# A new set-up ahead of a two-layer LSTM: other orders of loads, products and conversions on every queue

## The chip, the cores and the metric

One core of one Trainium2 chip. The metric is the device time of one execution in microseconds (us). The kernel before takes 1119.18 us (median of 3 runs, 1118.47 to 1119.56). "Before" and "after" are the kernel without and with the change; line numbers (L1069) are those of the kernel before.

## The reference, cut to what matters

2048 sequences of 10 steps. Table rows are looked up, projected and convolved over time; with a tanh'ed embedding they feed two LSTM layers (H = 256, 8 steps) and three dense layers without a nonlinearity between them.

```python
rp = concat([region_tbl[region_idx], poi_tbl[poi_idx]])          # (2048, 10, 12)
nv = concat([rp @ W_rp + b_rp, coords @ W_co + b_co])            # 40 features
conv = elu(conv1d(nv, conv_w) + conv_b)                          # 3 taps, 32 channels, 8 steps
emb = tanh(concat([car_tbl[car_idx], week_tbl[week_idx], time_tbl[time_idx]]))   # 27
x = concat([conv, broadcast(emb)])                               # (2048, 8, 59)
h = lstm_layer(x, Wih0, Whh0, ...); h = lstm_layer(h, Wih1, Whh1, ...)
y = ((h[:, -1] @ W1 + b1) @ W2 + b2) @ W3 + b3
```

## The kernel before, in words

The 2048 sequences are four batches of 512 columns. Ahead of the batches stands a **set-up**, written out by hand for each engine, that does once what all batches need. Then each engine walks through the same list of stages (`stages`): cells of layer 0 and layer 1 in turn, and between them the turning of gathered rows, the convolution and the embeddings' share of the gates of the next batch. A cell is 8 gate tiles (6 in a sequence's first step) of 128 rows by 512 columns; a recurrent tile is six fp16 matmuls (weights and states split into a high and a low part) after the input's matmul.

The set-up, on the tensor engine (PE), in its order: W1 turned (8 matmuls, L1233); the product W1·W2 in eight column blocks (`product_w12`, L1069, each 8 matmuls of 257 columns), with `band` between the fourth and fifth (24 small matmuls, L1109: projection folded into the convolution's weights); `product_conv_bias`; `poi_rows` (80 matmuls of 12 columns, L1130: batch 0's point-of-interest rows by a one-hot product); `turn_wx` (L1098: the input weights turned and scaled by a diagonal); batch 0's first rows turned and the first convolution half (`conv_pair(0)`, L1166), around `turn_wh(0)` (L1084: the recurrent weights of layer 0, four quarters of 8 matmuls); the embeddings turned; the **first cell**; the embeddings' gates (`emb_product`, L1174) between two head products (`product_head`, (W1·W2)·W3, L1139, 16 matmuls of 512 columns each); `conv_pair(1)`; `turn_wh(1)` and `turn_wh(2)`, layer 1's weights; `sum_head_bias`; the **second cell**, from which on the steady order runs.

The scalar engine (ACT) takes products out of the accumulators: `put_w12`, `put_wx_hi`, `put_wh_hi` (L624), `put_head_hi`, the convolution's elu parts, the cells' gates (L683), `put_emb_gates` (L666). The vector engine (DVE) does index arithmetic (`indices`), the one-hots, `row_maxima` (L780) and `row_scales` for the scaling diagonals, the low parts (`put_wh_lo` L814, `put_wx_lo`, `put_head_lo`), the rest of the elu, and the head bias sum (L845). SyncE (SP) issues the loads in order and then, in `put_pair`, the copies of the convolution's results into `x_in`: 12 DMAs for the first two steps, 12 for the next two. GpSimd (POOL) gathers table rows by indirect DMA (L527): batch 0's regions of four steps, after a wait the embeddings' rows, then the other steps.

What orders the engines is semaphores alone: each engine runs its own list in order, so a waiting instruction holds all behind it on its engine.

Of the kernel before, what the change touches and what calls it, by code (L numbers as in the profile page):

```python
# [33 lines left out]
SIDES = 2  # L34

# [132 lines left out]
def build(nc, d):  # L168
# [33 lines left out]
    with ExitStack() as ctx:  # L202
# [3 lines left out]
        def sem(name):  # L206
            return ctx.enter_context(nc.semaphore(name))

        idx_raw = {"region": sb("region_raw", [P, NB * GR, T], I32), "poi": sb("poi_raw", [P, NB * GR, T], I32),
                   "car": sb("car_raw", [P, NB * GR, 1], I32), "week": sb("week_raw", [P, NB * GR, 1], I32),  # L210
                   "time": sb("time_raw", [P, NB * GR, 1], I32)}
        idx_wrap = sb("idx_wrap", [P, NB * GR, T], F32)
        idx = {k: sb(f"{k}_idx", list(v.shape), F32 if k == "week" else I32) for k, v in idx_raw.items()}
# [40 lines left out]
        with ExitStack() as early:  # L254
            PAD = (WIN - 1) * D_FEAT
            proj_t = sb("proj_t", [D_NV, PAD + D_FEAT + PAD], F32, early)
            conv_w = sb("conv_w", [D_NV, TAPS, D_CONV], F32, early)
            proj_bias = sb("proj_bias", [D_NV, 1], F32, early)
            conv_b = sb("conv_b", [P, 1], F32, early)
            poi_sum = sb("poi_sum", [P, GR * T, D_POI], F32, early)  # L260
            poi_tbl = sb("poi_tbl", [P, D_POI], F32, early)
            poi_rest = sb("poi_rest", [P, 2, D_POI], F32, early)
            poi_part = sb("poi_part", [P, 3, D_POI], BF16, early)
            poi_number = sb("poi_number", [P, 2], F32, early)
# [28 lines left out]
        with ExitStack() as before_layer1:  # L293
            w_nat.extend(sb(f"w_nat{i}", [P, M, H], F32, before_layer1) for i in (1, 2))
            diag.append(sb("diag1", [P, M, P], F32, before_layer1))
            w12_t = sb("w12_t", [P, K2, H], F32, before_layer1)
# [12 lines left out]
        idx_in = {k: sem(f"{k}_in") for k in idx_raw}  # L309
        coords_in = sem("coords_in")  # L310
# [4 lines left out]
        proj_in, conv_bias_in = sem("proj_in"), sem("conv_bias_in")  # L315
# [7 lines left out]
        zeroed, proj_zeroed = sem("zeroed"), sem("proj_zeroed")  # L323
# [5 lines left out]
        poi_part_step, poi_part_put = sem("poi_part_step"), sem("poi_part_put")  # L329
# [5 lines left out]
        diag_ready, wh_acc, wh_hi_put, wh_lo_put = sem("diag_ready"), sem("wh_acc"), sem("wh_hi_put"), sem("wh_lo_put")  # L335
        wx_copied = sem("wx_copied")
        wx_acc, wx_hi_put, wx_lo_put = sem("wx_acc"), sem("wx_hi_put"), sem("wx_lo_put")
        emb_copied = sem("emb_copied")
        band_acc, band_put = sem("band_acc"), sem("band_put")
# [3 lines left out]
        head_acc, head_hi_put, head_low_put = sem("head_acc"), sem("head_hi_put"), sem("head_low_put")  # L343
        one_ready, head_sum_step, head_bias_acc, head_bias_put = (sem("one_ready"), sem("head_sum_step"),
# [10 lines left out]
        x_put = [sem("x0_put"), sem("x1_put"), sem("x2_put")]  # L355

# [26 lines left out]
        WH_BANKS = ((1, 2, 0, 1), (1, 0, 2, 1), (0, 2, 1, 3))  # L383
# [4 lines left out]
        PAIR_DMAS = 3 * PAIR * 2  # L388

        def x_count(part, n):  # L390

            return ((n * 3 + PAIR_DMAS) * DMA, (n * 3 * (TT - 1) + PAIR_DMAS) * DMA, (n + 1) * (3 * TT * DMA))[part]

# [23 lines left out]
        def put_pair(eng, s):  # L417
            for k in range(PAIR):
                for half in range(2):
                    row = (half * PAIR + k) * D_CONV  # L420
                    put_x(eng, s * PAIR + k, slice(row, row + D_CONV), slice(s * HALF, (s + 1) * HALF),
                          slice(half * HALF, (half + 1) * HALF), x_put[s])

        @block.sync
        def _(sp):
# [4 lines left out]
            def load_rows(k):  # L430
                load(idx_raw[k][:, :, :].rearrange("p (n g) t -> p n g t", g=GR),
                     d[f"r_{k}_idx"].rearrange("(n p g) t -> p n g t", p=P, g=GR), idx_in[k])
# [4 lines left out]
            load(w2[:, :, 0:D2 // 2], w2_rows[:, :, 0:D2 // 2], w2_in[0])  # L437
            for k in ("car", "time", "week"):
# [47 lines left out]
        def _(pool):  # L486
# [29 lines left out]
            for n in range(NB):  # L516
# [56 lines left out]
                else:  # L573

                    for c in range(CH):
                        pool.wait_ge(turned[c], n)
# [766 lines left out]
```

## Time and profile before

| | us |
|---|---|
| median of 3 runs | 1119.18 |
| the profiled execution: its time | 1118.79 |
| its span (first to last instruction) | 1117.0 |
| PE busy | 1076.6 (96%) |
| DVE, ACT, POOL busy | 743.0, 510.1, 319.9 |
| PE's first matmul of the second cell starts at | 102.10 |

The span is the stretch from the first to the last instruction; the time adds what lies around it (1.79 us). PE's busy time is summed over matmuls whose ends are modelled; a busy PE is not PE at its peak.

### The profile page before, as it was taken

The page shows a single profiled execution, that of the slowest core. Times are in us where ns is not written, and L with a number is a line of the kernel's source. Part 1 is how long each engine was busy: PE and PEld are TensorE (multiplying, and loading weights), DVE is VectorE, ACT ScalarE, POOL GpSimd, SP SyncE. Part 2 cuts the span into 40 slices and gives each one's busy share as a digit, 9 for nine tenths or more (in the row PEclk, how much of TensorE's full clock was granted, in tenths as well). Part 3 has the DMA queues.
Part 4 walks back from the last instruction along what each step waited for, and adds up shares of the span by engine and source line. Part 5 has one row for each costly group of instructions (what it writes and reads, how often), then busy time and mean ns, then how long its engine had stood idle before and what let it go on. Part 6 is the DMA issues. An engine that isn't in the chain of part 4 may idle for free.

```text
span 1117.0 us, 14516 instructions
## 1 busy us (share of the span) xinstructions
PE 1076.6 (96%) x4994; PEld 520.8 (47%) x4994; DVE 743.0 (67%) x1136; ACT 510.1 (46%) x735; POOL 319.9 (29%) x338
## 2 busy tenths in 40 slices
PE   5959999999999999999999999999999999999998
PEld 4835444444444544444444544444444544444444
DVE  1558858576676767666686768666676758666653
ACT  1334544444455544444455544444455545444432
POOL 6550025562540015562541015552442000000000
PEclk9779999999999999999999999999999999999999
DMA  9510001000010101000010101000010100000001
GB/s 224 144 17 15 1 2 30 3 2 1 2 31 1 40 2 31 3 2 1 2 30 2 40 1 29 5 2 1 2 30 1 38 1 21 9 0 1 0 1 38
DMA packets 34382, 22.59 MB, mean 20 GB/s; under 512 B 22922, under 2 KB 27018, under 8 KB 34186
## 3 DMA queue, kind: packets, MB, share of 16 engines
q1 hardware_dynamic: 21648, 20.54, 6.7%
q0 software_dynamic: 9984, 1.12, 2.6%
q8 instruction: 41, 0.67, 0.2%
q10 hardware_dynamic: 2682, 0.04, 0.2%
q14 instruction: 27, 0.22, 0.1%
HBM read 11.18 MB, written 4.19 MB: 14 GB/s over the span
## 4 chain that ended last, share of the span: by engine, by line
PE 93%; DVE 3%; issue 1%; DMA 1%; ACT 1%; SPq 1%; ACTq 0%; DVEq 0%
PE acc L1224 52%; PE acc L1215 28%; PE acc L1206 5%; PE acc L1069 2%; PE aux L1314 2%; PE acc L1139 1%; DMA w<-in_L_rec_W 1%; PE aux L1174 1%; SPq L413 1%; PE aux L1304 1%; ACT gates L683 1%; PE aux L1130 0%; PE aux L1098 0%; PE aux L1084 0%; DVE gates L925 0%
## 5 line engine op out<-in xcount | busy, mean ns | idle before, releaser
L1224 PE MATMUL acc<-h_part,wh 128*128 128x512 f16 (+1 forms) x2688 | 656.1, 380 | 1.6 <-DVE h_part L976 1.6
L1224 PEld LDWEIGHTS acc<-h_part,wh 128*128 128x128 f16 x2688 | 245.2, 98 | 322.0 <-issue 55.7
L1215 PE MATMUL acc<-h_part,wh 128*128 128x512 f16 (+1 forms) x1488 | 358.9, 379 | 0.4 <-issue 0.3
L683 ACT ACTIVATE gates<-acc,gate_bias,unscale 128x512 f32<-128x512 f32 x254 | 196.1, 777 | 328.9 <-PE acc L1224 278.0
L683 ACT ACTIVATE gates<-gates,gate_bias,unscale 128x512 f32<-128x512 f32 x242 | 190.2, 811 | 150.1 <-DVE gates L925 143.8
L1215 PEld LDWEIGHTS acc<-h_part,wh 128*128 128x128 f16 x1488 | 144.4, 98 | 178.2 <-issue 7.6
L527 POOL DMA_INDIRECT feat<-in_L_rec_region_tbl,region_idx x160 | 160.4, 1002 | 163.7 <-PE acc L1224 124.7
L925 DVE TENSOR_TENSOR gates<-acc,emb_gates 128x512 f32<-128x512 f32 x242 | 161.6, 686 | 54.9 <-PE acc L1224 46.3
L527 POOL DMA_INDIRECT feat<-in_L_rec_poi_tbl,poi_idx x120 | 121.7, 1014 | 114.5 <-PE acc L1224 96.9
L1206 PE MATMUL acc<-x_in,wx 96*128 96x512 f32 (+1 forms) x248 | 139.2, 567 | 15.7 <-DMA x_in<-conv_hi 11.9
L972 DVE TENSOR_TENSOR h_full<-gates,tanh_c 128x512 f32<-128x512 f32 x120 | 82.6, 688 | 75.8 <-ACT tanh_c L688 69.6
L951 DVE TENSOR_TENSOR cell_c<-gates,cell_c 128x512 f32<-128x512 f32 x112 | 76.8, 686 | 76.4 <-ACT gates L683 72.6
L946 DVE TENSOR_TENSOR ig<-gates 128x512 f32<-128x512 f32 x112 | 76.9, 687 | 67.2 <-ACT gates L683 64.3
L688 ACT ACTIVATE tanh_c<-cell_c 128x512 f32<-128x512 f32 x128 | 80.0, 625 | 59.9 <-DVE cell_c L954 42.2
L976 DVE TENSOR_TENSOR h_part<-h_full,h_part 128x512 f16<-128x512 f32 (+1 forms) x120 | 83.3, 694 | 16.0 <-DVE h_part L973 6.2
L954 DVE TENSOR_TENSOR cell_c<-cell_c,ig 128x512 f32<-128x512 f32 x112 | 77.5, 692 | 13.1 <-DVE cell_c L951 1.8
L973 DVE TENSOR_TENSOR h_part<-gates,tanh_c 128x512 f16<-128x512 f32 (+1 forms) x120 | 83.0, 692 | 0.0
L1206 PEld LDWEIGHTS acc<-x_in,wx 96*128 96x128 f32 x248 | 47.9, 193 | 47.1 <-issue 17.1
L539 POOL COPY feat<-coords 128x80 f32<-128x80 f32 x4 | 1.0, 252 | 220.9 <-PE aux L1152 218.4
L897 DVE RECIPROCAL neg_part<-neg_part 128x512 f32<-128x512 f32 (+1 forms) x9 | 27.0, 2997 | 0.3
L1314 PE MATMUL aux<-w_head,h_last 128*128 128x512 f32 x96 | 24.1, 404 | 0.6 <-DVE h_last L967 0.6
L944 DVE TENSOR_TENSOR cell_c<-gates 128x512 f32<-128x512 f32 x16 | 11.0, 689 | 14.7 <-ACT gates L683 13.5
(126 smaller groups left out, 375.4 us busy)
## 6 DMA issues: line engine op xcount, KB each, us to landing
out<-y SPq DMA_DIRECT2D x16, 256.0 KB, 2.6
x_in<-conv_hi SPq DMA_DIRECT2D x56, 64.0 KB
feat<-in_L_rec_region_tbl,region_idx POOLq DMA_INDIRECT x160
w<-in_L_rec_W SPq DMA_DIRECT2D x2, 1024.0 KB
w_nat<-in_L_rec_Whh SPq DMA_DIRECT2D x2, 1024.0 KB, 13.1
w<-in_L_rec_W SPq DMA_DIRECT2D x1, 2048.0 KB
feat<-in_L_rec_poi_tbl,poi_idx POOLq DMA_INDIRECT x120
x_in<-conv_lo SPq DMA_DIRECT2D x28, 64.0 KB
```

Source lines behind the costliest of these rows:

```text
L527: pool.indirect_dma_start(out, None, tables[k], bass.IndirectOffsetOnAxis(ap=idx[k][:, n * GR + g, t:t + 1], axis=0)).then_inc(landed, DMA)
L683: nc.scalar.activation(gates[layer][:, j, g, :], source, ACT.Tanh if g == GATE_G else ACT.Sigmoid, bias=gate_bias[:, layer, m:m + 1], scal ...
L688: nc.scalar.activation(tanh_c[layer][:, j, :], cell_c[layer][:, j, :], ACT.Tanh).then_inc(tanh_c_done[layer], 1)
L925: nc.vector.tensor_tensor(gates[0][:, j, g, :], acc[:, s.bank(j, g), :], emb_gates[:, g * HK + j, :], ALU.add).then_inc(gate_sum, 1)
L946: nc.vector.tensor_tensor(ig[:, j, :], i_gate, g_gate, ALU.mult).then_inc(ig_done[layer], 1)
L954: nc.vector.tensor_tensor(c, c, ig[:, j, :], ALU.add).then_inc(c_done[layer], 1)
L972: nc.vector.tensor_tensor(h_full[:, j, :], o_gate, th, ALU.mult).then_inc(h_full_done[layer], 1)
L973: nc.vector.tensor_tensor(hi, o_gate, th, ALU.mult).then_inc(h_hi_done[layer], 1)
L976: nc.vector.tensor_tensor(lo, h_full[:, j, :], hi, ALU.subtract).then_inc(h_done[layer], 1)
L1206: mm = nc.tensor.matmul(bank, wx[:, rows], x_in[:, s.t, :], start=True, stop=s.first and not s.opening)
L1215: mm = nc.tensor.matmul(bank, wh[:, 1, a, c, rows], h_part[0][:, s.write_slot, b, c, :], start=(c == 0 and a == b == HI), stop=(s.first an ...
L1224: mm = nc.tensor.matmul(bank, wh[:, own_w, a, c, rows], h_part[layer][:, s.read_slot, b, c, :], start=False, stop=(c == HK - 1 and a == LO))
```

## The change

The same work is computed with other instructions and another order in the set-up; the steady stages are as before. The parts:

- **Loads.** Batch 0's region indices and coordinates are loaded alone, the other batches' at the end of SP's loads. Rows are grouped by 128 neighbours (`"(g p) t -> p g t"`), so one partition's run of indices is 40 bytes. Car, time and week indices come as 16 rows of 512 bytes each, one tile of 96 rows, whose wrap-around is computed at once and which PE turns (`turn_small`). W2's two halves go together ahead of the poi indices; W3 goes ahead of the biases and of layer 1's weights.
- **Projection and band.** The weights are loaded in natural order three times on a diagonal and turned by PE (`turn_proj`); the band is 4 matmuls over all taps, and the convolution's bias one.
- **Poi rows.** 20 matmuls of 24 columns with a block-diagonal table.
- **W12.** ACT takes out all 257 columns in one copy; the bias is added by DVE once (`add_head_bias`). The order is blocks 0, 1, band, blocks 2 to 7.
- **Order on PE.** `turn_wh(0)` runs mostly ahead of the first rows' turning; both head products and `turn_wh(1)` run ahead of the first cell, all three `emb_product` parts and `turn_wh(2)` after it.
- **Order on DVE and ACT.** `row_maxima(1)` and `(2)` run after the first elu; layer 1's diagonal is built by ACT (8 activations) in place of one DVE instruction; the head bias sum is split in two; `elu(1)` runs after `put_wh_lo(2)`.
- **The opening's copies.** The first cell waits only for its own step's six copies (`x_put[0]`); the six of the second step have a semaphore of their own.
- **Gathers.** POOL issues the embeddings' gathers without waiting for the first 16 region gathers to land.
- **Index arithmetic** of batches 1 to 3 (region and poi, two rounds of three) stands after the second cell on DVE, where poi's one round stood.

```diff
@@ SP
-            load_rows("region")
+            load(idx_raw["region"][:, 0:GR, :], rows_of("r_region_idx", 0, GR), first_idx_in)
+            sp.wait_ge(small_zeroed, 1)
+            for k, at in (("car", CAR_AT), ("time", TIME_AT), ("week", DAY_AT)):
+                load(small_raw[at:at + NB * GR, :], d[f"r_{k}_idx"].rearrange("(g p) -> g p", p=P), small_idx_in)
             load(w1_nat[:, :, :], d["W1"].rearrange("(a p) n -> p a n", p=P), w1_in)
...
+            load(w3[:, :, :], d["W3"].rearrange("(k p) n -> p k n", p=P), w3_in)
...
+            load(idx_raw["region"][:, GR:NB * GR, :], rows_of("r_region_idx", GR, NB * GR), later_idx_in)
+            load(idx_raw["poi"][:, GR:NB * GR, :], rows_of("r_poi_idx", GR, NB * GR), later_idx_in)
+            load(coords[:, GR:NB * GR, :], coord_rows[:, GR:NB * GR, :], later_coords_in)
@@ POOL
                     copy_coords()
-                    pool.wait_ge(rows_first_in, GR * PAIR_WIN * DMA)
-                    pool.wait_ge(idx_ready, 3)
-                    gather_emb()
+                    pool.wait_ge(small_put, 1)
+                    gather_emb(0, GR)
                     copy_emb()
@@ ACT
+            def diagonal1():
+                act.wait_ge(prep, 9)
+                for m in range(M):
+                    nc.scalar.activation(diag[1][:, m, :], ident[:, :], ACT.Copy, scale=row_scale[:, 1, m:m + 1]
+                                         ).then_inc(diag_ready[1], 1)
...
             put_wx_hi()
+            put_wh_hi(0, 0, 3)
             put_turned(feat_t[0:KP, 0, :], aux[0:KP, 0, :], first_turned, 1, first_turned_put)
-            put_wh_hi(0, 0, 1)
+            put_wh_hi(0, 3, 4)
             elu_parts(0, slice(0, HALF))
-            put_wh_hi(0, 1, 4)
-            emb_tanhs(0, acc[:, 3, :])
-            act.wait_ge(prep, 4)
+            put_head_hi(0)
+            diagonal1()
+            put_head_hi(1)
+            emb_tanhs(0, acc[:, 0, :])
+            put_wh_hi(1)
             act.wait_ge(bias_ready, 1)
             first, second = opening_cells(STEPS)
             cell_acts(first)
-            put_emb_gates(0, 0)
-            put_head_hi(0)
-            put_emb_gates(0, 1)
+            for part in range(3):
+                put_emb_gates(0, part)
+            put_wh_hi(2)
             put_turned(feat_t[0:KP, 1, :], acc[0:KP, 0, :], turned[0], 1, turned_put[0])
-            put_head_hi(1)
             elu_parts(1, slice(0, HALF))
-            put_emb_gates(0, 2)
-            put_wh_hi(1)
-            put_wh_hi(2)
             cell_acts(second)
@@ DVE, the order after
+            indices(0, "region", REG, slice(0, GR), (first_idx_in, DMA))
+            small_indices()
             put_band()
+            put_conv_bias()
+            poi_parts()
             poi_one_hot()
             row_maxima(0)
             row_scales(0)
+            week_lookup()
             put_poi()
             put_wx_lo()
+            add_head_bias()
+            put_wh_lo(0)
...
             elu(0, slice(0, HALF), (0, slice(0, HALF)), ())
+            sum_head_bias(0, K2 // 2)
+            put_head_lo(0)
+            row_maxima(1)
+            row_maxima(2)
+            row_scales(1)
+            put_head_lo(1)
             split_emb(0)
+            put_wh_lo(1)
             first, second = opening_cells(STEPS)
             cell(first)
+            sum_head_bias(K2 // 2, K2)
+            put_wh_lo(2)
             elu(1, slice(0, HALF), (0, slice(HALF, NCOL)), ())
...
             cell(second)
-            indices(4, "poi", POI)
+            dve.wait_ge(x_second_put, HALVES_DMAS * DMA)
+            later = slice(GR, NB * GR)
+            indices(1, "region", REG, later, (later_idx_in, 2 * DMA))
+            dve.wait_ge(idx_ready, 2)
+            indices(2, "poi", POI, later, (later_idx_in, 2 * DMA))
@@ PE, the order after
+            turn_small()
...
+            turn_proj()
...
+            product_w12(0)
+            product_w12(1)
+            band()
+            for m in range(2, K2):
                 product_w12(m)
             poi_rows()
+            turn_wx([(band_put, 1), (conv_bias_put, 1), (conv_bias_put, 1), (poi_put, SIDES)])
+            turn_wh(0, [(wx_lo_put, 1), (wx_lo_put, 2), (wx_lo_put, 4)])
             pe.wait_ge(rows_first_in, GR * PAIR_WIN * DMA)
             pe.wait_ge(coords_put, 1)
+            pe.wait_ge(wh_lo_put, 1)
             turn_steps(aux[:, 0, :], 0, PAIR_WIN, first_turned)
+            turn_wh(0, [(wh_lo_put, 2)], begin=3)
...
             conv_pair(0)
+            product_head(0)
+            product_head(1)
             pe.wait_ge(emb_copied, 1)
+            turn_emb(acc[:, 0, :])
+            turn_wh(1, [(wh_lo_put, 3), (wh_lo_put, 4), (first_turned_put, 1), (relu_done, 1)])
             pe.wait_ge(emb_ready, 2)
             cell(first)
+            pe.wait_ge(wh_lo_put, 7)
+            for part in range(3):
+                if part:
+                    pe.wait_ge(emb_gates_put, EMB_BEFORE[part])
+                emb_product(0, part)
+            turn_wh(2, [(wh_lo_put, 8), (emb_gates_put, 5), (emb_gates_put, 7), (emb_gates_put, M)])
             pe.wait_ge(rows_in[0], rows_count(0, 0))
             turn_steps(acc[:, 0, :], PAIR, PAIR_WIN, turned[0])
+            sum_head_bias()
             pe.wait_ge(turned_put[0], 1)
+            pe.wait_ge(wh_lo_put, 9)
             conv_pair(1)
             cell(second)
```

In `cell`, the second cell's first three tiles wait for the first cell's gates or the turned rows, and its fourth (place 3) for `head_bias_put`, DVE's reading of that accumulator bank.

## Rows read from the trace of the kernel before

**Rows 1.** PE's longest wait behind 103 us: us in total, times, longest.
```profile
PE acc L1206 <- ACT gates L683: 2.7, 3, 0.9
```

**Rows 2.** Timeline of PE in the set-up: start us, elapsed us, engine, line.
```profile
7.58 1.94 PE L1233 MATMUL acc<-ident,w_nat 128*128 128x128 f32 x8 [7.58 <-DMA w_nat<-in_L_rec_W]
11.04 10.18 PE L1069 MATMUL acc<-w_t,w 128*128 128x257 f32 x32 [1.52 <-DMA w<-in_L_rec_W]
21.15 1.69 PE L1109 MATMUL aux<-conv_w,proj_t 40*84 40x32 f32 x19
...
27.89 8.61 PE L1069 MATMUL acc<-w_t,w 128*128 128x257 f32 x32
...
42.30 2.90 PE L1130 MATMUL aux<-poi_part,poi_hot 64*64 64x12 bf16 x46 [1.02 <-issue]
45.13 6.70 PE L1098 MATMUL aux<-diag,wx_rep 128*96 128x128 f32 x32
...
52.10 1.06 PE L1084 MATMUL aux<-diag,w_nat 128*128 128x128 f32 x8
...
69.82 0.76 PE L1206 MATMUL acc<-x_in,wx 96*128 96x512 f32 x1 [11.87 <-DMA x_in<-conv_hi]
...
75.80 7.03 PE L1139 MATMUL acc<-w,w_t 128*128 128x512 f32 x16
...
102.10 0.79 PE L1206 MATMUL acc<-x_in,wx 96*128 96x512 f32 x1
...
113.09 0.58 PE L1206 MATMUL acc<-x_in,wx 96*128 96x512 f32 x1
```

**Rows 3.** Timelines of SP and ACT: two loads, the input weights' copies.
```profile
1.25 0.50 SPq L428 DMA_DIRECT2D w_nat<-in_L_rec_W  x1
...
17.60 4.33 SPq L428 DMA_DIRECT2D coords<-in_r_coords  x1
...
36.95 1.64 ACT L700 COPY wx_rep<-wx_nat 128x768 f32<-128x768 f32 x2
```

**Rows 4.** Stretches: PE, PEld, DVE, ACT, POOL busy; PE clock, DMA share, GB/s.
```profile
30.00:32.00 2.00, 2.00 (x9) 1.65 (x9) 1.97 (x2) 0.54 (x2) 1.12 (x1) 0.82 0.61 5
...
46.00:48.00 2.00, 2.00 (x11) 2.00 (x10) 0.47 (x2) 0.58 (x1) 1.52 (x3) 0.50 0.00 0
...
60.00:62.00 2.00, 0.00 (x0) 0.00 (x0) 2.00 (x5) 0.00 (x0) 1.65 (x2) 0.86 0.13 21
...
78.00:80.00 2.00, 2.00 (x6) 0.90 (x5) 1.90 (x4) 0.24 (x1) 1.07 (x2) 1.00 0.00 0
```

**Rows 5.** Groups, 0 to 103 us: busy us, mean ns, idle.
```profile
L814 DVE TENSOR_TENSOR wh<-aux,wh 128x512 f16<-128x512 f32 x12 | 7.9, 686 | 1.5 <-ACT wh L624 1.5
L780 DVE TENSOR_REDUCE row_max<-w_nat 128x8 f32<-128x2048 f32 x3 | 6.8, 2280 | 0.0
L845 DVE SCALAR_TENSOR_TENSOR head_sum<-w,b,head_sum 128x512 f32<-128x512 f32 x7 | 5.3, 752 | 0.2
...
L683 ACT ACTIVATE gates<-acc,gate_bias,unscale 128x512 f32<-128x512 f32 x6 | 4.4, 774 | 11.8 <-PE acc L1209 11.8
L666 ACT COPY emb_gates<-aux 128x512 f32<-128x512 f32 x8 | 4.2, 594 | 0.0
...
L617 ACT ACTIVATE b<-acc,b_col 128x1 f32<-128x1 f32 x8 | 2.2, 270 | 0.0
```

**Rows 6.** Timeline of DVE: first elu's ends, the poi indices' last.
```profile
56.21 0.28 DVE L894 TENSOR_SCALAR neg_part<-tanh_part 128x256 f32<-128x256 f32 x1
...
59.62 0.43 DVE L911 TENSOR_TENSOR conv_lo<-relu_part,conv_hi 128x256 fp32r<-128x256 f32 x1
...
121.65 0.24 DVE L758 TENSOR_SCALAR poi_idx<-idx_wrap 128x160 int32<-128x160 f32 x1
```

**Rows 7.** Timeline of POOL: the copy that follows the embeddings' gathers.
```profile
45.74 0.51 POOL L555 COPY emb<-emb 128x384 f32<-128x384 f32 x1 [4.41 <-DMA emb<-in_L_rec_time_tbl,time_idx]
```

**Rows 8.** Timeline of PE behind the second cell: the only stall there.
```profile
129.37 0.49 PE L1206 MATMUL acc<-x_in,wx 96*128 96x512 f32 x1 [0.46 <-DVE gates L925]
```

More of the change, by code:

```diff
@@ L418, in put_pair @@
             for k in range(PAIR):
+                put = x_put[1] if s else (x_put[0], x_second_put)[k]
                 for half in range(2):
@@ L541, in copy_coords, with gather_emb @@
                                           ).then_inc(coords_put, 1)
-                def gather_emb():
-                    for g in range(GR):
-                        gather("car", emb[:, g, 0, 0:D_CAR], g, 0, emb_rows_in)
-                        gather("time", emb[:, g, 0, D_CAR + D_WEEK:D_EMB], g, 0, emb_rows_in)
+                def gather_emb(begin, end):
+                    for g in range(begin, end):
+                        for k, at, cols in (("car", CAR_AT, slice(0, D_CAR)),
+                                            ("time", TIME_AT, slice(D_CAR + D_WEEK, D_EMB))):
+                            at += n * GR + g
+                            gather(k, emb[:, g, 0, cols], small_idx[:, at:at + 1], emb_rows_in)
                 def copy_emb():
@@ L615, in put_w12 @@
                 act.wait_ge(w12_acc, m + 1)
-                nc.scalar.copy(w12_t[:, m, 0:H], bank[:, 0:H]).then_inc(w12_put, 1)
-                nc.scalar.activation(b12[:, m:m + 1], bank[:, H:H + 1], ACT.Identity,
-                                     bias=b2_col[:, m:m + 1]).then_inc(w12_put, 1)
+                nc.scalar.copy(w12_t[:, m, :], bank[:, 0:H + 1]).then_inc(w12_put, 1)
             def put_wh_hi(i, begin=0, end=len(QUARTERS)):
@@ L1102, in turn_wx, with turn_small, turn_proj @@
                     mm.then_inc(wx_acc, 1)
+            def turn_small():
+                pe.wait_ge(small_ready, 1)
+                nc.tensor.transpose(acc[:, 3, 0:SMALL], small_wrap[:, :], ident[0:SMALL, 0:SMALL]
+                                    ).then_inc(small_turned, 1)
+            def turn_proj():
+                rows, cols = BIAS_AT + 1, TAPS * D_NV + 1
+                pe.wait_ge(proj_in, (2 * TAPS + 2) * DMA)
+                nc.tensor.transpose(aux[0:cols, 1, 0:rows], proj_nat[:, :], ident[0:rows, 0:rows]
+                                    ).then_inc(proj_turned, 1)
@@ L1111, in band @@
                 mm.then_inc(band_acc, 1)
[L1113 to L1119 removed]
+                nc.tensor.matmul(aux[:, 1, P:P + 1], conv_w[:, :, :].rearrange("k s o -> k (s o)"), proj_bias[:, :],
+                                 start=True, stop=True).then_inc(conv_bias_acc, 1)
```

313 lines of the change are left out of this document (160 added, 153 removed).

## The prediction

> **What bounds the kernel now.** I read PE's waits behind the set-up first, since the change leaves the steady stages alone. The longest sum there is 2.7 us in a thousand [rows 1]: from the second cell on PE is never short of work, so every microsecond by which that cell starts earlier or later moves the end by about as much. The question is therefore one number, the start of the second cell, 102.10 before [rows 2].
>
> Next PE's timeline of the set-up [rows 2]. Three things are to be seen in it. First, small matmuls are dear: `band` has 24 of them, 19 take 1.69 us together and the rest stretch to 27.89, 6.7 us from 21.15, with the engine idle and waiting for nothing that the profile names ("issue"); `poi_rows` has 80 and ends at 45.13, though its last 46 ran in 2.90. Second, a hole from about 58 to 69.82: the first elu and twelve copies into `x_in`, 11.87 us of idle [rows 2]. Third, two head products of 7.03 us each stand behind that hole, in front of the second cell. Then the clock [rows 4]: full (2.4 GHz) in 78 to 80 with PE busy, half (1.2 GHz) in 46 to 48 although PE is busy, after the sparse poi rows, and falling in 60 to 62 after PE had been idle since 58.
>
> The sum below is made in the profiled execution's own time: 1118.79 us, 0.39 under the median of the three runs, span 1117.0.
>
> **Stage A: from the start to the last of `turn_wx`** (51.8 before: 45.13 + 6.70).
> - W1's load is issued behind three more loads at 0.50 each [rows 3], so PE turns W1 from about 8.9 in place of 7.58 and W12 starts at 12.2 (before 11.04). This is a loss of 1.2. `turn_small` (one matmul) ends before W1 lands; `turn_proj` is one more.
> - A 512-column fp32 product costs 7.03/16 = 0.44 us a matmul at full clock, so 257 columns cost 0.22 at full and 0.43 at half. Before, 32 took 10.18 [rows 2], about half of them at 0.43. After, I put all 16 of blocks 0 and 1 at 0.43: 6.9, to 19.1.
> - `band` and bias: 4 + 1 products, 10 matmuls (fp32 goes in two) at 0.09 (1.69/19): 0.9, to 20.0. Bounds: 0.9, and 0.9 + 3.8 if the idle pieces of before come back.
> - Six blocks at full clock: 48 x 0.22 = 10.3, to 30.5. DVE's line beside it: band copy, poi parts, one-hots, `row_maxima(0)` 2.28 [rows 5] and the diagonal end some 11 us behind the band, at 31, in time.
> - `poi_rows`: 20 matmuls. The nearest row is 46 in 2.90, 0.06 each, with 64 by 64 tiles at half clock; for twice the width I take 0.10, 2.0 us, beside ACT's last W12 copy and the two copies of the input weights, 0.6 + 1.64 [rows 3]. `turn_wx` starts at 33.
> - `turn_wx`, 32 matmuls: 6.70 before at half clock; 4 x 1.06 = 4.2 at full, by the eight of `turn_wh` [rows 2]. I expect the clock to hold, since PE's gaps are now short. With 1.8 kept for idle pieces of the kind above, the stage ends at T = 39. Bounds: 37.4 without them, 45 with both old stalls and the half clock. Gain in A: 12.8.
>
> **Stage B: from T to the second cell** (50.3 before: 51.8 to 102.1). Times are after T.
> - `turn_wh(0)`'s three quarters 3.2, first rows turned 3.8, last quarter 4.9, `conv_pair(0)` 5.5. ACT's three activations to 6.6, DVE's elu 3.84 (56.21 to 60.05, [rows 6]) to 10.5. Before, the elu ended at 60.05, 8.3 behind 51.8: the four low parts that now stand ahead of it cost 2.
> - This loss is covered. PE does both head products meanwhile: 5.5 + 2 x 7.0 = 19.4. The copies of the first step land at about 10.5 + 6 x 0.64 + 2.6 = 17 (an estimate from the 9.8 us that the twelve took from 60.05 to 69.82 [rows 2]). The hole is gone; what is late next is layer 1's diagonal.
> - DVE behind the elu: half of the head sum 2.9 (0.75 each), a low part 0.7, two maxima 4.6 [rows 5], scales 1.1: 19.8. ACT's 8 activations of 128x128: between 0.27 (one column) and 0.59 (512 columns) each [rows 5], I take 0.28: 2.2 (bounds 2.2 and 4.7), to 22.0. PE idles 2 us there. `turn_wh(1)` 4.2 to 26.2.
> - ACT takes out those quarters until 26.8, then six gates at 0.77 and two tanh: 5.5, to 32.3. PE's first cell ends at 28.8; the first part of `emb_product` at 29.5; the next needs banks that ACT empties after its gates: 3 x 0.51, 33.9. In this gap of 4.4 us the clock falls, as it did 4 us into the hole at 60 to 62 [rows 4]. Parts 2 and 3, then `turn_wh(2)` at 1.6 a quarter (6.70/4, the half clock's price) in place of 1.06: to 43. Turned rows, bias sum, `conv_pair(1)`: second cell at 44.5. Bounds: 42.2 (clock held) and 48 (dear activations too).
> - Gain in B: 50.3 - 44.5 = 5.8.
>
> **Behind the start, two losses.** `elu(1)` now stands ahead of DVE's reading of the head bias's bank. ACT's parts end at about 45.5, the elu 3.84 later, the bias 0.68 after it, at 50, whereas PE wants that bank for place 3 at 44.5 + 3 x 1.57 = 49.2 (a tile is a seventh of 113.09 - 102.10, [rows 2]): 0.8 to 1.2 lost; I take 1.1. DVE's index arithmetic behind the cell is two rounds where one ended at 121.89 [rows 6]; PE was already short of DVE by 0.46 at 129.37 [rows 8], so the added round, 0.7 to 1.0, goes straight into that stall: 0.8.
>
> **Cost nothing.** The wait that POOL drops: without it the embeddings' gathers start some 2 us earlier (a guess: the coordinates, which POOL copies first, land at about 28). Their copy was ready at 46.25 [rows 7], and PE turns them at T + 19.4 = 58. With the wait left in, it would be ready 12 us early all the same. The waits between later steps stay; the second turning is at 81. W3 and layer 1's weights: 10.6 MB landed by 46 before, and the maxima want theirs at 53.
>
> Sum: 12.8 + 5.8 - 1.1 - 0.8 = 16.7. 1118.79 - 16.7 = 1102.1 profiled, **1102.5** against the median.
>
> **Rivals.**
> 1. *The idle pieces come back* (they are the loads' traffic in PE's way, not the count of small matmuls): band + 3.8, `poi_rows` + 2.7 less the 1.8 allowed, half clock in `turn_wx` + 2.5, some 1.5 more for blocks at half clock: 8.7 less gained, 1111. For it: they stand where DMA is busiest, and it is as busy after. Against: the big matmuls of W12 show none in the same traffic. Chance 0.13.
> 2. *Everything holds*: no idle pieces (1.6 to 1.8 more) and no fall of the clock in B (2.3 more): 1098.4. Chance 0.13.
> 3. *Slower: late weights of layer 1.* `turn_wh(1)` now stands in front of the first cell, so Wih1 and Whh1, which end SP's weights behind W3 and the biases, must land before anything goes on. Each us beyond T + 14 = 53 costs one; slower than before from a landing at 53 + 17 = 70, and at 75 the time is 1124. For it: row loads of short runs choke SP (coordinates in 80-byte runs held it for 4.33, [rows 3]) and 30 to 32, in the biases' 4-byte runs, moved 5 GB/s [rows 4]. Against: DMA was idle at 46 to 48 with the same bytes [rows 4], 22 us short of the point. Chance 0.04.
>    The Trainium skill, "DMA: Bandwidth & Descriptors", Specifications, says that a transfer wants 512 B at least for line rate. The change goes from 160-byte runs to 40-byte ones for the indices, which speaks against it. The slump at 30 to 32 agrees in kind. By that page alone, with each of the 4,608 late runs (1,536 each for region, poi and coordinates) charged as 512 B, they are 2.4 MB, an estimate of 8 us; they stand behind all weights, so the sum is the same unless their like stands ahead.
> 4. *The change does nothing for the end*, because the second cell's start is tied to something that I don't see: 1118 to 1120. Chance 0.02.
>
> **How the numbers follow.** The forecast has 0.68. Its own range is 1097.5 to 1107 from the bounds: T + 3 or - 1.6, B + 3 or - 2.3. To hold the time 8 times in 10, I reach to the first rival's near side: 1097 to 1110. What a measurement can tell from no change is 0.2%, 2.2 us. Faster: 0.68 + 0.13 + 0.13 = 0.94; same 0.02; slower 0.04.
>
> **What would show it.** In the profile after: the last of `turn_wx` at 37 to 41; head products side by side from about 44 to 58 and no hole for `x_in` ahead of the first cell; about 2 us of idle PE ahead of `turn_wh(1)`; half clock in `turn_wh(2)`; the second cell at 83 to 84, with about 1 us of idle at its fourth tile; a stall of about 1.3 us where 129.37 stood. Wrong would be a second cell later than 90 or earlier than 79, a wait for a weights' DMA, or a gather that ends a wait of PE.

## The result, and the profile after

| | median us | lowest to highest | runs |
|---|---|---|---|
| before | 1120.03 | 1118.34 to 1121.56 | 20 |
| after | 1115.78 | 1105.89 to 1119.75 | 20 |

The ratio is 0.9959, 95% interval 0.9945 to 0.9972: faster, by 4.3 us, where 16.7 was forecast (1102.5, range 1097 to 1110). Eighteen of the 20 executions of the changed kernel took 1114.76 to 1119.75; the other two took 1105.89 and 1109.16, and have no trace. The profiled execution took 1114.92 us, span 1113.1.

PE's timeline of the set-up after the change (start us, elapsed us, engine, line, operation; in brackets the idle time before it and what ended it). It answers to [rows 2].

```profile
9.63 6.10 PE L1144 MATMUL acc<-w_t,w 128*128 128x257 f32 x16
...
20.21 1.30 PE L1196 MATMUL aux<-conv_w,proj_t 120*84 120x32 f32 x8 [4.47 <-issue]
...
21.75 8.02 PE L1144 MATMUL acc<-w_t,w 128*128 128x257 f32 x29
...
34.14 0.38 PE L1144 MATMUL acc<-w_t,w 128*128 128x257 f32 x1 [2.42 <-issue]
...
39.66 6.46 PE L1144 MATMUL acc<-w_t,w 128*128 128x257 f32 x16 [5.14 <-ACT w_t L658]
45.95 1.27 PE L1209 MATMUL aux<-poi_block,poi_hot 128*128 128x24 bf16 x20
48.12 3.77 PE L1173 MATMUL aux<-diag,wx_rep 128*96 128x128 f32 x32 [0.89 <-ACT wx_rep L740]
...
73.75 3.81 PE L1159 MATMUL aux<-diag,w_nat 128*128 128x128 f32 x32 [2.49 <-issue]
...
85.18 0.96 PE L1253 MATMUL aux<-emb_in,we 128*128 128x512 f32 x3 [4.11 <-ACT emb_gates L706]
...
88.35 5.96 PE L1159 MATMUL aux<-diag,w_nat 128*128 128x128 f32 x32
...
96.11 0.49 PE L1289 MATMUL acc<-x_in,wx 96*128 96x512 f32 x1
...
101.85 0.49 PE L1289 MATMUL acc<-x_in,wx 96*128 96x512 f32 x1 [0.84 <-DVE b_head L1105]
```

`turn_wx` ends at 48.12 + 3.77 = 51.9, as before (51.8), and not at 39. The second cell starts at 96.11, 6.0 earlier. In the prediction's two stages: A gained nothing (12.8 forecast), B takes 44.2 in place of 50.3 (44.5 forecast). Behind the second cell the span goes on for 1017.0 where it was 1014.9: 2.1 lost, 1.9 forecast.

Why A is long is seen on the other engines: first ACT's and VectorE's timelines after the change, then POOL's.

```profile
16.60 0.37 ACT L658 COPY w_t<-acc 128x257 f32<-128x257 f32 x1 [2.81 <-PE acc L1144]
39.14 1.20 ACT L658 COPY w_t<-acc 128x257 f32<-128x257 f32 x4 [22.17 <-remote]
```

```profile
29.23 0.29 DVE L884 COPY conv_band<-aux 84x128 f32<-84x128 f32 x1 [23.37 <-remote]
32.06 0.16 DVE L888 COPY conv_bias<-aux 128x1 f32<-128x1 f32 x1 [2.54 <-remote]
```

```profile
23.55 0.94 POOL L549 DMA_INDIRECT feat<-in_L_rec_region_tbl,region_idx  x1 [0.30 <-issue]
25.32 0.25 POOL L561 COPY feat<-coords 128x80 f32<-128x80 f32 x1 [0.83 <-issue]
25.73 0.97 POOL L549 DMA_INDIRECT emb<-in_L_rec_car_tbl,small_idx  x1 [0.16 <-issue]
...
34.49 2.59 POOL L549 DMA_INDIRECT emb<-in_L_rec_time_tbl,small_idx  x1 [0.30 <-issue]
```

ACT takes W12's third block only at 39.14 and then four at once, although PE had finished that block by about 25; "remote" says that the profile finds nothing on this core that it waited for. VectorE copies the band, done at 21.5, at 29.23. PE, out of accumulator banks, stands still for 5.14, and for 2.42 with nothing named ("issue"). I call these the *pieces*: idle time for which the profile names no cause on this core. POOL's gathers now run from 4.67 to 37.08, with no break longer than the 1.24 us between the two rows of gathers. The same marks were in the profile of before, and I had passed over them: ACT's third block copy was late there by a "remote" too, but came at 27.62, 2.7 us behind POOL's last region gather (24.95) (its row, kernel before):

```profile
27.62 0.37 ACT L616 COPY w_t<-acc 128x256 f32<-128x256 f32 x1 [8.63 <-remote]
```

### The profile page after: what moved, and what is told of

Same layout as the page of the kernel before. It is cut to its first block, busy times and chain, and to the rows that moved or that the text cites. A ratio compares the mean times of both kernels' runs of the same rounds, so it can differ in the third digit from the quotient of the medians.

```text
span 1113.1 us, 14344 instructions
## 1 busy us (share of the span) xinstructions
PE 1071.6 (96%) x4898; PEld 515.2 (46%) x4898; DVE 741.6 (67%) x1146; ACT 510.7 (46%) x737; POOL 319.5 (29%) x339
## 3 DMA queue, kind: packets, MB, share of 16 engines
q10 hardware_dynamic: 2327, 0.08, 0.2%
## 4 chain that ended last, share of the span: by engine, by line
PE 86%; DVE 5%; issue 2%; SPq 2%; another core or an unknown queue 2%; ACT 2%; DMA 1%; DVEq 0%; ACTq 0%
PE acc L1307 48%; PE acc L1298 25%; PE acc L1289 5%; SPq L428 2%; PE aux L1396 2%; PE acc L1218 1%; PE acc L1144 1%; PE aux L1159 1%; DVE neg_part L967 1%; ACT gates L723 1%; PE aux L1253 1%; DVE h_full L1042 1%; DVE h_part L1043 1%; DVE gates L995 1%
## 5 line engine op out<-in xcount | busy, mean ns | idle before, releaser
L1289 PEld LDWEIGHTS acc<-x_in,wx 96*128 96x128 f32 x248 | 47.1, 190 | 38.9 <-issue 7.0
L1144 PE MATMUL acc<-w_t,w 128*128 128x257 f32 x64 | 21.7, 506 | 8.8 <-ACT w_t L658 5.1
```

Source lines behind the costliest of these rows:

```text
L1289: mm = nc.tensor.matmul(bank, wx[:, rows], x_in[:, s.t, :], start=True, stop=s.first and not s.opening)
```

## The experiments

Eighteen runs were made on four chips, A to D. This can't be left out: the kernel before took 1119.8 us on A, 1107.7 on B, 1107.7 and 1108.1 in the two sets on C, and 1120.7 on D. Which chip gave the result above is not on record; its kernel before took 1120.0, as on A and D. Only C was used in two sets, so a cause that came with a set and not with the chip is not excluded. Each ratio is to the kernel before in the same set; edits are to the changed kernel. T is the end of `turn_wx`, S the start of the second cell, both from the one execution that was profiled; the us are medians of four to six executions (e10: one).

### Chip A: traffic, the biases, POOL's wait, conv_w

```diff
# e1_hold: ahead of W3's load, SP's queue
+            sp.wait_ge(w12_put, K2)
# e2_bias_runs: the biases in runs of 128 B, not 4 B, into other places
-                    load(bias_in[:, layer, i, :], d[f"{k}{layer}"].rearrange("(m p) -> p m", p=P), bias_loaded)
+                    row = (layer * 2 + i) * 32
+                    load(bias_in[row:row + 32, :, :, :].rearrange("p a b m -> p (a b m)"),
+                         d[f"{k}{layer}"].rearrange("(a b) -> a b", b=32), bias_loaded)
# e3_wait_back: ahead of gather_emb(0, GR)
+                    pool.wait_ge(rows_first_in, GR * PAIR_WIN * DMA)
# e4_conv_w_first: conv_w's and conv_b's loads first on ACT's queue
```

> The changed kernel with one added wait: SP issues W3 and everything behind it (biases, layer 1's weights, later rows) only once ACT has taken out all eight W12 blocks. Theory F (in the changed kernel ACT, DVE and PE stand still between 17 and 39 us because what they need next of their own code arrives late while the loads keep the DMA engines busy; ACT takes out the third W12 block at 39.1 though PE had it done at about 24): DMA falls quiet at about 26 us, ACT's third copy comes at 24 to 30, turn_wx ends at 38 to 44, the time is 1101 to 1108. Rival D (the 4,096 four-byte bias runs choke the rings; they come later here too): the same gain at the front. Rival S (ACT's late copies have to do with its own place in the order and not with traffic): ACT's third copy stays at 35 or later and the time at 1114 or above, since the loads are now later still.

> The changed kernel with the four bias loads as 32 runs of 128 bytes each in place of 1,024 of 4 bytes, into other places of the tile (the gate biases are not those of the reference); all else as it was, W3 still ahead. Theory F: bulk bytes stay the same, so ACT's idle before its third W12 copy stays above 8 us, the time moves by less than 5 us (1111 to 1116). Rival D (small runs, not bytes): ACT's third copy comes before 30 and the time falls to 1103 to 1108.

> The changed kernel with POOL's wait for the first 16 region gathers put back ahead of the embeddings' gathers. The prediction's step (this wait costs nothing, hidden by 12 us): ratio to the changed kernel within 0.3%, 1113 to 1118, embeddings' copy still bound by DVE's day lookup at 44 us. Rival (gathers that pile up in the rings are what holds the others' code back): the time moves by more than 5 us and ACT's idle before its third W12 copy shrinks by as much.

> The changed kernel with the convolution's weights as the first two loads of ACT's queue, ahead of b1 and the projection. PE idles 4.5 us ahead of the band (15.7 to 20.2) and no releaser is named. Theory C (that wait is for the convolution's weights, whose 128-byte runs share the DMA engines with the poi indices' 10 KB runs): the band starts at 15.8 to 16.5 and the 4.5 us of idle are gone. If C is the whole cause of the late stage A, the time falls to 1105 or less; if theory F holds beside it, ACT's copies stay late (behind 33 us) and the time falls by 0 to 5 us. Theory F alone: the band still waits until about 20.

| | us | ratio, interval | T | ACT's third block |
|---|---|---|---|---|
| e1_hold | 1114.26 | 0.9939 [0.9917, 0.9962] | 50.9 | 39.07 |
| e2_bias_runs | 1114.83 | 0.9963 [0.9951, 0.9975] | 51.1 | 39.10 |
| e3_wait_back | 1107.53 | 0.9901 [0.9885, 0.9917] | 43.9 | 27.95 |
| e4_conv_w_first | 1112.79 | 0.9919 [0.9889, 0.995] | 51.5 | 38.93 |

e2 leaves the biases in the wrong places, so its gates are computed with other numbers than the reference's; it serves for its time alone. e1 and e4 scatter as the changed kernel does: e1 from 1107.51 to 1116.12, e4 from 1103.92 to 1117.90, and e4's trace is of its slowest execution.

The traffic of W3, the biases and layer 1's weights is not the cause: e1 takes it out of that stretch (windows of 28 to 34 us, after and then e1: us, busy time of PE, PEld, VectorE, ACT and POOL, PE's clock, DMA share, GB/s), and ACT is as late. What e1 leaves is the traffic up to about 25 us (192 GB/s from 18 to 25). Nor are the biases' short runs the cause.

```profile
28.00:34.00 6.00, 2.52 (x11) 1.76 (x10) 1.89 (x11) 0.00 (x0) 4.53 (x5) 1.00 0.88 155
```

```profile
28.00:34.00 6.00, 3.37 (x15) 2.30 (x13) 3.13 (x11) 0.00 (x0) 4.53 (x5) 0.93 0.11 5
```

POOL's wait makes the difference: with it T is 43.9 and the time 1107.53, 5 to 7 us under its neighbours, and its ratio's interval (0.9885 to 0.9917) lies clear of that of the changed kernel in the result (0.9945 to 0.9972). It is not clear of e4's, whose executions scatter most. ACT's, POOL's, VectorE's and PE's timelines of e3:

```profile
27.95 0.65 ACT L659 COPY w_t<-acc 128x257 f32<-128x257 f32 x2 [10.28 <-PE acc L1145]
```

```profile
24.91 0.25 POOL L561 COPY feat<-coords 128x80 f32<-128x80 f32 x1 [0.42 <-issue]
30.07 2.80 POOL L549 DMA_INDIRECT emb<-in_L_rec_car_tbl,small_idx  x1 [4.90 <-DMA feat<-in_L_rec_region_tbl,region_idx]
```

```profile
27.82 0.29 DVE L885 COPY conv_band<-aux 84x128 f32<-84x128 f32 x1 [21.95 <-remote]
...
37.19 1.22 DVE L863 TENSOR_TENSOR diag<-ident,row_scale 128x1024 f32<-128x1024 f32 x1
```

```profile
38.52 5.40 PE L1174 MATMUL aux<-diag,wx_rep 128*96 128x128 f32 x32 [2.79 <-issue]
```

ACT is back 3.5 us behind the last region gather (24.49), and before the gathered rows have all landed, for which POOL waits until 30.07. A piece is left: VectorE's band copy comes at 27.82, so its chain ends with the diagonal at 38.41, and `turn_wx` starts right behind that, 2.8 us late and then partly at the half clock (5.40 us; 3.77 in e9 below). In e4 the 4.5 us of idle ahead of the band are gone, so they were conv_w's late landing, but in the execution profiled the pieces take all of it back (PE and ACT of e4):

```profile
16.02 0.72 PE L1196 MATMUL aux<-conv_w,proj_t 120*84 120x32 f32 x8
```

```profile
38.93 1.20 ACT L658 COPY w_t<-acc 128x257 f32<-128x257 f32 x4 [19.29 <-remote]
```

### Chip B: other pauses

```diff
# e5_pause_for_act: between region rows' and embeddings' gathers
+                    pool.wait_ge(w12_put, 3)
# e6_pause_early: the same wait after 12 of the 16 region gathers
# e7_gathers_late: ahead of all of POOL's gathers
+                    pool.wait_ge(w12_put, K2)
# e8_busy_pause: no wait; between the gathers 14 chained
+                        nc.gpsimd.memset(busy[:, :], 0.0).then_inc(busy_step, 1)
```

> The changed kernel with POOL waiting, between the region gathers and the embeddings' gathers, until ACT has taken out three W12 blocks. Theory P (ACT, and DVE too, get what they stand still for only while POOL pauses in its row of gathers; a pause of about 2.7 us is enough): ACT's third copy comes at 27 to 28.5 in place of 39.1, POOL's embeddings' gathers start right behind it, the time is 1105 to 1109 as with the old wait. Rival T (the third copy comes when the gathers' rows have landed, whatever POOL does): the third copy comes at 30 or later. Rival W (the old wait helps by the later start of the embeddings' gathers themselves, for DMA): time above 1110.

> The changed kernel with a pause of POOL after 12 of the 16 region gathers, at about 19.6 us, until ACT has taken out three W12 blocks; no pause behind the 16. Theory P: ACT is free at 22 to 23 and its third copy comes as soon as PE has the block, at 24 to 26, DVE's band copy at 21.5 to 23 in place of 27.8 or 29.2; the time is 1101 to 1107. Rival T or W (landing, or the embeddings' gathers): ACT's third copy not before 27.6, and the time 1107 or above.

> The changed kernel with all of POOL's gathers held until ACT has taken out all eight W12 blocks. Theory P at its purest: no idle of ACT or DVE is left in the first 30 us that is not explained by PE or a load (band copy 0.1 us behind the band, third copy as soon as the block is done, eighth at 31 to 34). The rows then come late: 16 gathers until about 53, landed at 56, so the first convolution waits for them and the time is 1108 to 1116. Rival F (the loads' traffic alone holds the engines): ACT's third copy still at 28 or later.

> The changed kernel with 14 chained clears of a spare tile of 256 columns on POOL between the two rows of gathers, about 5 us, so that POOL is busy there but issues no gather. If it is POOL's gathers that hold the others (their descriptors), ACT's third copy comes at 27 to 28.5 and the time is 1106 to 1110, as with the old wait; if it is any work of POOL, ACT's third copy stays at 38 or later and the time is at 1114 or above.

| | us | ratio, interval | T | S |
|---|---|---|---|---|
| e5_pause_for_act | 1100.72 | 0.9937 [0.9924, 0.9951] | 40.2 | 83.69 |
| e6_pause_early | 1102.11 | 0.9948 [0.9934, 0.9961] | 40.6 | 84.68 |
| e7_gathers_late | 1118.19 | 1.0095 [1.008, 1.011] | 40.1 | 101.31 |
| e8_busy_pause | 1101.35 | 0.994 [0.9924, 0.9957] | 40.3 | 83.81 |

No piece is in any of the four traces, and in e5 and e8 none is there even before POOL's pause begins at about 25, so they settled nothing about pauses. They raised the question whether this chip has pieces at all. What e7 shows is the price of too late a gather (its PE timeline), the case in which POOL's rows become the bound:

```profile
56.85 1.06 PE L1232 MATMUL aux<-ident,feat 128*56 128x128 f32 x4 [14.11 <-DMA feat<-in_L_rec_region_tbl,region_idx]
```

### Chip C: both kernels without the pieces

Unaltered: the changed kernel (e9), the kernel before (e10, one execution), e5 again (e11) and e3 again (e12).

> The changed kernel itself, unaltered, run beside the kernel before, the kernel with the old wait and the kernel with POOL's pause, all on one chip, because the kernel before took 1119.8 us on the chip of the first four experiments and 1107.7 on that of the next four. Theory G (POOL's unbroken row of gathers itself holds up the other engines' instructions: ACT's third block copy came at 39 and not at 25): wherever this runs, ACT's copy is again near 39, turn_wx ends at 51 to 52, and it is 8 to 12 us above the two kernels with a pause: ratio 0.995 to 0.997 on a chip like the first, about 1.003 on one like the second. Rival H (the hold-up is the chip's, not the gathers'): on a chip like the second ACT's copy comes at 25, turn_wx ends at 40 to 41 with no pause at all, the time is within 2 us of the kernels with a pause, about 1101, ratio 0.994; on a chip like the first it is 1114 to 1116 as before.

> The kernel before, unaltered, for its trace on this chip. Both theories: on a chip like the first turn_wx ends at 51.8 and there are pieces of idle time of PE in the set-up's first 40 us (ACT's copy 8.63 us behind, VectorE's conv_bias 3.07). Rival H: on a chip like the second (time near 1107.7) these pieces are absent, and turn_wx ends some 10 to 12 us earlier, at 40 to 42; Theory G keeps turn_wx at 48 to 52 and must find the 12 us elsewhere.

> The changed kernel with POOL waiting for ACT's third block copy (w12_put at 3) between the region rows' gathers and the embeddings', as once before, now on the same chip as the changed kernel. Theory G: ACT's copy at 25 to 28, turn_wx ends at 40 to 44, ratio 0.989 to 0.994 and 8 us or more under the changed kernel. Rival H: equal to the changed kernel within 2 us, in whichever state the chip puts both; on a chip like the first ACT's copy would then be late and the time 1112 or more.

> The changed kernel with the old wait back (POOL waits until the region rows have landed before the embeddings' gathers), now beside the changed kernel. Theory G: 6 to 10 us under the changed kernel, as the 8 us measured before. Rival H: that 8 us was the chip's own scatter; equal to the changed kernel within 2 us.

| | us | ratio, interval | T | S | span behind S |
|---|---|---|---|---|---|
| before (e10) | 1106.6 | | 40.5 | 89.96 | 1014.8 |
| after (e9) | 1101.05 | 0.9941 [0.9927, 0.9954] | 40.5 | 84.10 | 1015.2 |
| e11, pause for ACT | 1100.62 | 0.9929 [0.9916, 0.9943] | 39.8 | 84.10 | 1014.7 |
| e12, old wait | 1101.7 | 0.9946 [0.9932, 0.9959] | 39.8 | 83.06 | 1014.7 |

PE of the kernel before on this chip, then PE and ACT of the changed kernel:

```profile
11.64 8.83 PE L1069 MATMUL acc<-w_t,w 128*128 128x257 f32 x32 [1.97 <-ACT w_t L693]
20.40 1.98 PE L1109 MATMUL aux<-conv_w,proj_t 40*84 40x32 f32 x24
22.31 7.22 PE L1069 MATMUL acc<-w_t,w 128*128 128x257 f32 x32
...
30.01 4.92 PE L1130 MATMUL aux<-poi_part,poi_hot 64*64 64x12 bf16 x80
34.86 5.69 PE L1098 MATMUL aux<-diag,wx_rep 128*96 128x128 f32 x32
...
57.90 0.76 PE L1206 MATMUL acc<-x_in,wx 96*128 96x512 f32 x1 [10.21 <-DMA x_in<-conv_hi]
```

```profile
20.25 1.30 PE L1196 MATMUL aux<-conv_w,proj_t 120*84 120x32 f32 x8 [5.35 <-DMA conv_w<-in_L_rec_conv_b]
...
21.80 12.88 PE L1144 MATMUL acc<-w_t,w 128*128 128x257 f32 x48
34.52 1.28 PE L1209 MATMUL aux<-poi_block,poi_hot 128*128 128x24 bf16 x20
36.69 3.77 PE L1173 MATMUL aux<-diag,wx_rep 128*96 128x128 f32 x32 [0.89 <-ACT wx_rep L740]
```

```profile
25.61 0.37 ACT L658 COPY w_t<-acc 128x257 f32<-128x257 f32 x1 [10.29 <-PE acc L1144]
```

Compare with [rows 2]: the 24 small `band` matmuls take 1.98 here and 6.7 there, the 80 poi matmuls 4.92 in one run. So the idle between them is no property of the matmuls: the same instructions run without it here. And T is the same for both kernels here too, because the changed one waits 5.35 for conv_w and then begins W12's 48 at the half clock (1.2 GHz; 12.88 us for all 48, where e14 below took 10.69). A window of e9, columns as above:

```profile
20.00:24.00 4.00, 3.75 (x15) 3.39 (x16) 1.98 (x11) 0.00 (x0) 3.09 (x4) 0.50 1.32 235
```

That is the price of the gap ahead of it. The wait that POOL dropped makes no difference on this chip: e12's interval and the changed kernel's overlap.

### Chip C again: conv_w

> conv_w's and conv_b's loads first on ACT's queue, and POOL waiting for ACT's third block copy between the two rows of gathers. Theory (two separate losses in stage A: conv_w's late load, 5.35 us of PE's idle time ahead of the band, and, on a chip that shows them, the idle pieces, about 8 us): on a chip like the second turn_wx ends at 36 to 37 (40.5 less some 4 to 5, as the band then starts at 15 to 16) and the time is 4 us under the changed kernel, 1096 to 1098, ratio 0.990; on a chip like the first turn_wx ends at 38 to 40, ratio 0.986. Rival (W12's last rows of W3 or ACT's copies end later than PE and take its place): turn_wx stays at 39 to 41, ratio 0.9935.

> conv_w's and conv_b's loads first on ACT's queue, no pause: as e4, now on this chip. Theory: on a chip like the second it equals e13 (no pieces to lift), 4 us under the changed kernel's 1101; on one like the first it is 1110 to 1114, far above e13. Rival: no better than the changed kernel, ratio 0.994.

> The changed kernel with fourteen chained memsets on POOL between the region rows' gathers and the embeddings', now perhaps on a chip that shows the idle pieces. If only the pause in the gathers counts: as the old wait, ratio 0.989 to 0.991 there. If POOL must stand still: ACT's third copy waits until 38 to 40 and the ratio is 0.994 to 0.997. On a chip like the second: 0.994 as before, which tells nothing of it.

> The changed kernel with POOL waiting for ACT's third block copy between the two rows of gathers. On a chip like the first: ACT's copy at 27 to 29, turn_wx at 42 to 45, ratio 0.989 to 0.992 as the old wait gave. On a chip like the second 0.993 to 0.994.

| | us | ratio, interval | T | S |
|---|---|---|---|---|
| e13, conv_w first and e5's pause | 1096.11 | 0.9897 [0.9882, 0.9912] | 35.9 | 79.37 |
| e14, conv_w first alone | 1095.68 | 0.9899 [0.9884, 0.9914] | 34.6 | 78.05 |
| e15, as e8 | 1100.89 | 0.9937 [0.9923, 0.995] | 40.3 | 84.36 |
| e16, as e5 | 1100.57 | 0.9937 [0.9923, 0.995] | 39.8 | 83.06 |

PE of e14:

```profile
17.33 0.72 PE L1196 MATMUL aux<-conv_w,proj_t 120*84 120x32 f32 x8
...
18.10 10.69 PE L1144 MATMUL acc<-w_t,w 128*128 128x257 f32 x48
28.63 1.28 PE L1209 MATMUL aux<-poi_block,poi_hot 128*128 128x24 bf16 x20
30.80 3.77 PE L1173 MATMUL aux<-diag,wx_rep 128*96 128x128 f32 x32 [0.89 <-ACT wx_rep L740]
```

Two loads moved to the front of ACT's queue are worth 5 us on this chip (e14 against e15 and e16): the wait is gone, and W12's 48 run at full clock (granted clock 1.00 from 12 to 28), with no gap of PE ahead of them. The price is small: the projection's weights now come behind them, and W12 begins at 10.99 in place of 9.84. These are the fastest times of any kernel here.

### Chip D: both kinds of pause where there are pieces

> conv_w's loads first on ACT's queue and POOL's pause until ACT's third block copy, as e13, once more, in the hope of a chip that shows the idle pieces. There: the two losses of stage A both go, turn_wx ends at 38 to 41, ratio 0.985 to 0.988. If the pieces come anyway, turn_wx ends at 48 to 50 and the ratio is 0.992 to 0.995. On a chip like that of e13: 0.9897.

> Fourteen chained memsets on POOL between the two rows of gathers, as e8 and e15. On a chip that shows the idle pieces: ratio 0.989 to 0.992 if only the pause in the gathers counts, 0.994 to 0.997 if POOL must stand still. On the other kind: 0.994.

| | us | ratio, interval | T | S |
|---|---|---|---|---|
| e17, as e13 | 1110.2 | 0.9898 [0.9881, 0.9915] | 43.8 | 89.60 |
| e18, as e8 | 1109.92 | 0.99 [0.9885, 0.9915] | 38.9 | 92.40 |

ACT and POOL of e17:

```profile
27.82 0.93 ACT L659 COPY w_t<-acc 128x257 f32<-128x257 f32 x3 [9.57 <-remote]
```

```profile
24.87 0.25 POOL L561 COPY feat<-coords 128x80 f32<-128x80 f32 x1 [0.34 <-DMA coords<-in_r_coords]
28.46 0.97 POOL L549 DMA_INDIRECT emb<-in_L_rec_car_tbl,small_idx  x1 [3.34 <-ACT w_t L659]
```

ACT, VectorE and POOL of e18:

```profile
27.71 0.93 ACT L667 COPY w_t<-acc 128x257 f32<-128x257 f32 x3 [11.69 <-remote]
...
42.99 0.59 ACT L680 CAST we<-aux 128x512 fp32r<-128x512 f32 x1 [2.27 <-remote]
```

```profile
20.70 0.29 DVE L893 COPY conv_band<-aux 84x128 f32<-84x128 f32 x1 [14.83 <-issue]
```

```profile
25.05 7.56 POOL L595 MEMSET busy<- 128x256 f32 x14
33.02 0.98 POOL L553 DMA_INDIRECT emb<-in_L_rec_car_tbl,small_idx  x1 [0.41 <-POOL busy L595]
```

The pieces are back with the chip. With either pause ACT resumes at 27.7 to 27.8, some 3.2 us behind the last region gather (24.5). POOL need not stand still for this: e18's is busy with memsets all that time. What ACT does on D without a pause was not run. e18 also has a piece (42.99) inside the second row of gathers, and its S is later than e17's although its T is 4.9 earlier: with the later second row there are pieces in stage B. e17's expectation (T at 38 to 41, ratio 0.985 to 0.988) was missed. Conv_w's gain is not seen in it, although its band was done at 17.1: VectorE takes the band out only at 27.69, its diagonal ends at 38.3, and `turn_wx` starts at 38.43, as in e3. In e18 VectorE did so at 20.70, and T is 4.9 earlier. The two edits of e17 together and the pause of e18 alone give the same ratio.

## Why the prediction was wrong

**What failed: stage A's last line, "With 1.8 kept for idle pieces of the kind above, the stage ends at T = 39"** (51.9 measured). The second cell came at 96.11, past the 90 that I had set as a sign of being wrong. Three things were wrong in that line.

1. *Whose the idle pieces were.* I tied them to the small matmuls of `band` and `poi_rows` and removed them with these. They don't belong to these matmuls: the same `band` costs 6.7 us in [rows 2] and 1.98 on C. There T was 40.5 in the kernel before already; 11.3 of the 12.8 that I counted as gain were time that the same kernel doesn't take on C. Rival 1 had the sign right (they come back) but named the loads' traffic; e1 excludes it for the stretch from about 25 us on, not for the time before.
2. *"With the wait left in, it would be ready 12 us early all the same."* I priced POOL's dropped wait by the data alone. True on C (e12: no difference), wrong on A: leaving the wait in gives T = 43.9 and 1107.53 there, inside my range. That is 8 us of the missing 12.9 in T, and 6.5 us in the ratio (0.9901 against 0.9959), shown by e3 against the changed kernel's own interval and against e1 and e2. The two pauses on D (ratios 0.9898 and 0.9900) agree. So one part of the change, the dropped wait between the gathers, takes back most of what the shorter set-up gives on such a chip.
3. *conv_w.* Nothing in my sum asks when the band's operands land. They are issued at 5.2 to 6.4 on ACT's queue and land at 20.2 (5.35 of idle in e9); first on the queue PE doesn't wait for them and T falls by 5.9, to 34.6. ACT's queue moved 2327 packets with 0.08 MB in the first 30 us of e9 beside SP's 5859 with 7.32 MB. The Trainium skill, "DMA: Bandwidth & Descriptors", Queues, rings and completion order, says that a DMA engine takes turns between queues packet by packet; by that, a queue of tiny packets waits for one of SP's each time. This case's trace agrees: from 10 to 20.2 us of e9, while both queues had work, ACT's moved 881 packets and SP's 897, one for one if the profile counts the packets that the page means. The single turns are not in the trace.

**The terms of A on a chip without pieces** (e9): W12 begins at 9.84 (12.2 forecast; I charged 1.2 for the loads ahead of W1, and it came 1.2 earlier than before), blocks 0 and 1 took 5.07 (6.9), six blocks 12.88 (10.3; 10.69 in e14), poi rows 1.28 (2.0), `turn_wx` 3.77 (4.2). The wait for conv_w took 5.35 (nothing), band and bias some 1.6 (0.9). T = 40.5 against 39. The forecast of the changed kernel was near, with errors that offset one another; the start of the comparison was not.

**Slips in the working.** 48 x 0.22 is 10.6, not 10.3, which moves nothing that matters. By its own bounds (T up to 45, B up to 48) the range should have reached 1112 and not 1107; that would still not have held 1115.78. The loads had moved 10.2 MB by 46, not 10.6. The 8 us in rival 3 go by a rate of about 300 GB/s that the sentence doesn't give.

**Stage B was right**: 44.2 (forecast 44.5), and 43.6 on C, against 50.3 and 49.4 before; its terms came out too. The hole for `x_in` is gone; the idle ahead of `turn_wh(1)` is 2.49 (2 forecast), its eight diagonals on ACT 2.44 together (2.2), the gap behind the first part of `emb_product` 4.11 (4.4), and `turn_wh(2)` runs at half clock, 5.96 (6.4).

**Behind the start**: the head bias's bank costs 0.84 at place 3 (1.1 forecast). The index rounds show as 0.41 and 0.55 where 0.46 stood, so 0.5 (0.8). The total in the trace of the result was 2.1, but there PE also waits 4.5 us in three places for `x_in`'s DMA, where before it waited 2.7 for ACT's gates [rows 1]; in e9 that wait for `x_in` is 0.6 and the total 0.4. So this sum was right partly by luck.

**Rivals 3 and 4**: PE never waits for layer 1's weights; rival 3 is out. Rival 4 (no effect) is out for the whole but is what stage A did.

**Stays open.** What holds ACT, VectorE and PE while POOL gathers, and why chips A and D show it and B and C not. It isn't every instruction: VectorE's band copy came at 29.23 amid the second row, and in e18 at 20.70 amid the first. Nor is it the end of the gathers that frees ACT: in four kernels with no pause (the changed one, e1, e2, e4) it resumed at 38.93 to 39.14, while the last gather ended at 37.08, 38.05, 35.00 and 37.90, so between 1.0 and 4.1 us behind it. The longest, ACT and POOL of e2:

```profile
39.10 1.20 ACT L660 COPY w_t<-acc 128x257 f32<-128x257 f32 x4 [22.19 <-remote]
```

```profile
34.05 0.95 POOL L551 DMA_INDIRECT emb<-in_L_rec_time_tbl,small_idx  x1 [0.30 <-issue]
```

That a pause lets ACT go is shown; that the gathers themselves hold it is argued. One theory on record, that the engines' next code arrives late, leaves no mark: the traces of the changed kernel, e2, e3 and e4 hold no packet of an instruction queue between 0.5 and 41 us. That does not rule it out. Nor is it known why single executions of kernels without a pause (1105.89, e1's 1107.51, e4's 1103.92) came out as fast as e3. The changed kernel itself was not run in the same set as e3, nor e5 on A.

## What to carry to other kernels

- Idle time that the profile ascribes to nothing ("issue", "remote") is no part of the work beside it. Before pricing its removal, see it in a second trace on another chip; here the same kernel differed by 11.3 us up to the end of `turn_wx`.
- A wait with no data reason may still break up a row of GpSimd gathers, and one that costs nothing by its data is not free to drop. In this set-up with its 24 gathers the pause cost nothing on one kind of chip (e12) and was worth 8 us of T, 6.5 of the time, on the other (e3): try both.
- When a stage is packed, ask of each small operand when its load lands: the 60 KB of `conv_w`, tenth in its queue, cost 5 us on C (e14). On D no gain of it is seen, since another engine was later still (e17).

## What the runs showed of the hardware

- The same program takes 1107.7 or 1120 us by the chip, and most of the difference stands in the set-up: T 40.5 against 51.8, while the span behind the second cell is 1014.8 and 1014.9.
- On the slower chips ACT stood still for up to 22.19 us (e2), the last 14 of them with its input ready, and VectorE for up to 24.72 (e2), the last 9. Most of that fell into GpSimd's gathers, one per 1.25 us, but ACT's went on for 4.1 us behind the last of them. In the four kernels with a pause (before, e3, e17, e18) ACT went on 2.7 to 3.5 us behind the last gather ahead of the pause.
- Two queues with work at once moved packets one for one: 881 of ACT's and 897 of SP's from 10 to 20.2 us (e9), though SP's carried nearly all the bytes.
- 4 fp32 products appear as 8 matmuls and 1 as 2 (`band` and the bias, e9).
